# A four-layer convolution network on one core: first layer's window loads in four pieces, its outputs stored by group, its input loads in halves, the last layer's weight tables made later

## The reference, cut to what matters

```python
def _conv_reflect(x, w, bias, dil, pad):
    xp = jnp.pad(x, ((0, 0), (0, 0), (pad, pad), (pad, pad)), mode='reflect')
    out = jax.lax.conv_general_dilated(xp, w, window_strides=(1, 1), padding='VALID', rhs_dilation=(dil, dil), ...)
    return out + bias[None, :, None, None]

def _denoise_block(x, w1, b1, w2, b2, w3, b3, a, b, c):
    trip = _triplets(x)            # channels t-1, t, t+1
    ...
    o = a * _conv_reflect(xf, w1, b1, 1, 2) + b * _conv_reflect(xf, w2, b2, 2, 4) + c * _conv_reflect(xf, w3, b3, 4, 8)
    return jnp.tanh(o).reshape(B, T, H, W)
y = _denoise_block(x, blk1_...)
z = _denoise_block(y, blk2_...)
```

## Time and profile before

| | us |
|---|---|
| median of 3 runs | 5447.36 |
| fastest, slowest | 5419.58, 5452.12 |
| the profiled execution | 5428.8 |
| its span from the first to the last instruction | 5426.9 |
| TensorE busy in it | 5009.2 (92%) |
| VectorE busy | 3375.0 (62%) |
| ScalarE busy | 2396.5 (44%) |
| GpSimd busy | 1336.2 (25%) |

### The profile page before, as it was taken

How to read it: one execution, slowest core, us unless ns; L and a number is a source line. 1 busy time by engine, 2 the same in 40 slices (tenths; PEclk the granted TensorE clock), 3 DMA queues, 4 the chain that set the end, 5 groups by cost and what they waited for, 6 DMA issues and landing times. The chain is left out here.

```text
span 5426.9 us, 176472 instructions
## 1 busy us (share of the span) xinstructions
PE 5009.2 (92%) x78653; PEld 2747.5 (51%) x78653; DVE 3375.0 (62%) x6195; ACT 2396.5 (44%) x2999; POOL 1336.2 (25%) x1245
## 2 busy tenths in 40 slices
PE   4999999999999999999999997999677799999998
PEld 2444444445454555555544543443555566666665
DVE  4555554555543544444444445888899788888888
ACT  1222222222221111111111116785899698988997
POOL 0022222222221100000000000000677355555556
PEclk9999999999999999999999998999999999999999
DMA  8888889988977667667667667999688466666664
GB/s 241 228 236 261 245 244 251 260 237 258 255 216 209 192 188 201 180 178 205 177 175 203 179 183 245 328 325 319 242 307 310 142 148 152 152 151 152 151 151 121
DMA packets 328769, 1166.61 MB, mean 215 GB/s; under 512 B 49641, under 2 KB 50280, under 8 KB 276202
## 3 DMA queue, kind: packets, MB, share of 16 engines
q1 hardware_dynamic: 325848, 1152.94, 74.1%
q10 hardware_dynamic: 2162, 2.39, 0.2%
HBM read 683.58 MB, written 453.51 MB: 210 GB/s over the span
## 5 line engine op out<-in xcount | busy, mean ns | idle before, releaser
L679 PE MATMUL c_p<-c_w,wc 128*32 128x512 f16 x55296 | 3043.8, 380 | 130.3 <-issue 116.2
L679 PEld LDWEIGHTS c_p<-c_w,wc 128*32 128x32 f16 x55296 | 1551.3, 97 | 1594.2 <-issue 199.3
L739 ACT ACTIVATE c_t<-c_p,cbias,cscale 128x512 f32<-128x512 f32 x512 | 397.9, 777 | 2625.2 <-PE c_p L679 2625.2
L601 DVE TENSOR_TENSOR a_x<-c_t,a_x 128x512 f32<-128x512 f32 x256 | 181.1, 707 | 877.1 <-ACT c_t L739 865.2
L1697 PE MATMUL f_P<-f_qh,f_wt 64*64 64x512 f16 x4608 | 545.7, 378 | 1.8 <-DVE f_t L1593 1.8
L1697 PE MATMUL f_P<-f_hl,f_wt 64*64 64x512 f16 x4608 | 545.3, 379 | 0.0
L591 DVE TENSOR_SCALAR c_y<-c_t 128x512 f16<-128x512 f32 x256 | 116.7, 456 | 682.1 <-ACT c_t L739 681.9
L1858 POOL TENSOR_TENSOR f_y<-f_y,f_x 128x512 f32<-128x512 f32 x256 | 330.7, 1292 | 448.9 <-DVE f_hl L1572 442.8
L1593 DVE SCALAR_TENSOR_TENSOR f_t<-f_P,f_kk,f_ci 128x256 f32<-128x256 f32 x1024 | 423.4, 475 | 12.6 <-PE f_P L1697 7.3
L1457 POOL TENSOR_TENSOR e_hl<-e_g,e_hl 128x2048 f16<-128x2048 f32 x63 | 257.2, 4083 | 607.5 <-ACT e_hl L1407 607.5
L1658 PE MATMUL f_qp<-f_hil,f_gT 128*128 128x260 f16 (+1 forms) x3120 | 390.9, 275 | 4.0 <-DVE f_qh L1577 4.0
(11 more groups left out here) (263 smaller groups left out, 5981.7 us busy)
## 6 DMA issues: line engine op xcount, KB each, us to landing
c_w<-ys SPq DMA_DIRECT2D x144, 1056.0 KB, 11.9
c_w<-xs SPq DMA_DIRECT2D x140, 1056.0 KB, 12.2
d_x<-x SPq DMA_DIRECT2D x128, 1024.0 KB, 7.8
x<-d_x SPq DMA_DIRECT2D x128, 1024.0 KB, 5.1
ys<-c_y SPq DMA_DIRECT2D x576, 132.0 KB, 9.8
xs<-a_hl SPq DMA_DIRECT2D x70, 1056.0 KB, 9.7
a_x<-in_x SPq DMA_DIRECT2D x256, 256.0 KB, 10.1
a_x<-in_x SPq DMA_DIRECT2D x128, 512.0 KB, 4.6
```

What stands on the lines that cost most here:

```text
L679: t = p.matmul(pg[32 * j:32 * j + 32, :], wu[:, blk, wl, var, di, :], buf[:, bk, xl * PW + PAD + dx:xl * PW + PAD + dx + NW], start=(di == ...
L739: s.activation(tt_[n % 3][:, :], pp[:, n % 4, :], ACT.Tanh, bias=cbias[:, blk:blk + 1], scale=cscale[:, blk:blk + 1]).then_inc(c_act, 1)
```

## The change

Five edits, all in `layer0`:

1. `load(u, g)` loads a quarter of the window (four bands, 264 KB per DMA) and may start when TensorE is done with group g of unit u - 2. SP asks for it in group g of its iteration; in even units of block 1 all four are asked for at g = 3. TensorE still waits for all four at group 0.
2. `store_y(u, g)` stores group g of a unit as soon as its edges are mirrored: all four strips in one DMA per channel and place. The number of DMAs (eight or twelve per unit) and their size (132 KB) stay. GpSimd mirrors each group by itself.
3. `store_x1(u, g)` stores block 2's output by group, two DMAs of 128 KB instead of four of 256 KB per unit and 1 MB: eight per unit.
4. `load_x` is split into two halves of four DMAs, in the even and the odd unit of a pair.
5. `table_of(u)` = u - 60: the tables are made in units 60 to 123, and each is stored in the next unit.

```diff
-            return u - 8 if 0 <= u - 8 < 64 else None
+            return u - 60 if 0 <= u - 60 < 64 else None
...
-                    if u < NU:
-                        hv = yt[u % 2][:, :, :, :].rearrange("p r l w -> p (r l) w")
-                        q.wait_ge(c_lo, 4 * u + 4)
+                        if u < NU:
+                            hv = yt[u % 2][:, g]
+                            q.wait_ge(c_lo, 4 * u + g + 1)
...
-                def load(u):
+                def load(u, g):
                     if u >= 2:
-                        e.wait_ge(c_pe, 4 * (u - 1))
+                        e.wait_ge(c_pe, 4 * (u - 2) + g + 1)
...
-                            e.dma_start(win[half][gp % 2 + 2 * h8:128:4].rearrange("p k w -> p (k w)"),
-                                        dram(src, pair(b, gp, 0, 16 * half) + h8 * (8 * VP - RW), [[CP, 16], [RW, 2], [1, 16 * RW]])).then_inc(c_ld[half], 16)
+                            e.dma_start(win[half][gp % 2 + 2 * h8:128:4, 4 * g:4 * g + 4].rearrange("p k w -> p (k w)"),
+                                        dram(src, pair(b, gp, 0, 16 * half + 4 * g) + h8 * (8 * VP - RW),
+                                             [[CP, 16], [RW, 2], [1, 4 * RW]])).then_inc(c_ld[half] if u else c_l0[g // 2], 16)
...
-                def store_y(u):
-                    e.wait_ge(c_pad, 2 * (u + 1))
-                    for j in (0, 2, 1, 3):
-                        y = yt[u % 2][32 * j:32 * j + 32].rearrange("p r l w -> p r (l w)")
-                        for m, gp, slot in [(0, p, 1), (1, p + 1, 0)] + [(1, 0, 0)] * (p == 0) + [(0, 8, 1)] * (p == 7):
-                            e.dma_start(dram(ys, pair(b, gp, slot, 16 * half + j), [[VP, 16], [4 * RW, 4], [1, RW]]), y[m::2]).then_inc(c_yd[u % 2], 16)
+                def store_y(u, g):
+                    e.wait_ge(c_pad, 8 * u + 2 * g + 2)
+                    y = yt[u % 2][:, g].rearrange("p l w -> p (l w)")
+                    for m, gp, slot in [(0, p, 1), (1, p + 1, 0)] + [(1, 0, 0)] * (p == 0) + [(0, 8, 1)] * (p == 7):
+                        e.dma_start(dram(ys, pair(b, gp, slot, 16 * half) + g * 4 * RW, [[RW, 4], [VP, 16], [1, RW]]), y[m::2]).then_inc(c_yd[u % 2], 16)
...
+                def store_x1(u, g):
+                    for m in range(2):
+                        e.dma_start(dram(x1[b], (2 * p + m) * 4 * NW + (2 * half + g // 2) * NW + g % 2 * 64 * 4 * NC * NW,
+                                         [[4 * NC * NW, 64], [1, NW]]), xwin(u)[m::2, g]).then_inc(c_1d[u % 2], 16)
...
                 for u in range(2 * NU):
+                    late = u < NU and half == 0
                     for g in range(4):
                         i, s = stage_of(u, g)
                         if s == 3:
                             store_xs(i)
+                        if u + 2 < 2 * NU and not late:
+                            load(u + 2, g)
+                        if u + 2 < 2 * NU and late and g == 3:
+                            for gg in range(4):
+                                load(u + 2, gg)
+                        if blk:
+                            store_x1(u, g)
+                        else:
+                            store_y(u, g)
+                        if g == 0 and NU <= u + 1 < 2 * NU:
+                            load_res(u + 1)
+                        if g == 1 and u // 2 + 4 < NG:
+                            load_x(u // 2 + 4, (half,))
+                        if g == 2 and u and table_of(u - 1) is not None:
+                            store_table(table_of(u - 1))
```

More of the change, by code:

```diff
@@ L379, in n_win @@
         def n_win(u):
-            return 32 * sum(1 + (place(r)[2] == 0) for r in range(u % 2, u + 1, 2) if r)
+            return 128 * sum(1 + (place(r)[2] == 0) for r in range(u % 2, u + 1, 2) if r)
         def table_of(u):
-            return u - 8 if 0 <= u - 8 < 64 else None
+            return u - 60 if 0 <= u - 60 < 64 else None
         def xwin(u):
@@ L817, in load_x @@
                         e.wait_ge(a_lo, i - 1)
-                    for c, r in ((c, r) for c in range(2) for r in range(4)):
+                    for c, r in ((c, r) for c in channels for r in range(4)):
                         e.dma_start(xin[i % 2][:, c, NW * r:NW * r + NW],
@@ L832, in load @@
                     if u >= 2:
-                        e.wait_ge(c_pe, 4 * (u - 1))
-                    elif u == 1:
+                        e.wait_ge(c_pe, 4 * (u - 2) + g + 1)
+                    elif u == 1 and g == 0:
                         e.wait_ge(a_v, mark["wc"])
@@ L855, in load_res @@
                         e.wait_ge(c_mm, 8 * (r - 1))
-                        e.wait_ge(c_1d[u % 2], 64 * (r // 2))
+                        e.wait_ge(c_1d[u % 2], 128 * (r // 2))
                     else:
@@ L860, in load_res, with store_table @@
                         e.dma_start(xwin(u)[m::2], rows(x, u, m, NW, NH * NW)).then_inc(c_xd[u % 2], 16)
[L862 removed]
+                def store_y(u, g):
                     blk, b, p, half = place(u)
[L864 to L875 removed]
+                    e.wait_ge(c_pad, 8 * u + 2 * g + 2)
[3 more added lines that the diff above has]
+                def store_x1(u, g):
+                    e.wait_ge(c_lo, 4 * u + g + 1)
+                    blk, b, p, half = place(u)
+                    for m in range(2):
+                        e.dma_start(dram(x1[b], (2 * p + m) * 4 * NW + (2 * half + g // 2) * NW + g % 2 * 64 * 4 * NC * NW,
+                                         [[4 * NC * NW, 64], [1, NW]]), xwin(u)[m::2, g]).then_inc(c_1d[u % 2], 16)
+                def store_table(ht):
+                    e.wait_ge(w_t, 6 * (ht + 1))
+                    e.dma_start(K.wtab[ht], wt[ht % 2][:, :]).then_inc(w_td[ht % 2], 16)
                 load_x(0)
@@ L893, in _ @@
                 store_xs(1)
-                load(0)
-                load(1)
+                for u in range(2):
+                    for g in range(4):
+                        load(u, g)
                 load_x(3)
@@ L901, in _ @@
                     blk, b, p, half = place(u)
-                    nxt = (u + 1) // 2 + 2
+                    late = u < NU and half == 0
                     for g in range(4):
@@ L906, in _ @@
                             store_xs(i)
-                    if NU <= u + 1 < 2 * NU:
-                        load_res(u + 1)
-                    if u + 2 < 2 * NU:
-                        load(u + 2)
-                    if blk:
-                        store_x1(u)
-                    else:
-                        store_y(u)
-                    if table_of(u) is not None:
-                        ht = table_of(u)
-                        e.wait_ge(w_t, 6 * (ht + 1))
-                        e.dma_start(K.wtab[ht], wt[ht % 2][:, :]).then_inc(w_td[ht % 2], 16)
-                    if half == 0 and nxt + 2 < NG:
-                        load_x(nxt + 2)
+                        if u + 2 < 2 * NU and not late:
[13 more added lines that the diff above has]
+                            store_table(table_of(u - 1))
                 for q in range(2):
-                    e.wait_ge(c_1d[q], 64 * (NU // 2))
+                    e.wait_ge(c_1d[q], 128 * (NU // 2))
                     e.wait_ge(w_td[q], 16 * 32)
```

16 lines of the change are left out of this document (3 added, 13 removed).

## The result

| | before | after |
|---|---|---|
| median of 4 runs, us | 5437.55 | 5385.02 |
| lowest, highest | 5419.58, 5452.12 | 5374.08, 5391.84 |
| span of the profiled execution | 5426.9 | 5383.9 |
| block 1 (first activation of unit 0 to last of unit 63) | 1635.6 | 1659.3 |
| block 2 (to the last of unit 127) | 1569.2 | 1503.7 |

The ratio after to before is 0.990 (0.9879 to 0.992): 1.0% faster. 5507 us was forecast, 1.1% slower; the measured time lies in the range of 5380 to 5690 us, but the kernel got faster, not slower.

The account below looks back on a forecast made before the run. TensorE bounds both blocks before; after, four DMA engines were to bound block 1 at 1740 us. 5426.9 + 104 (block 1) - 45 (block 2) = 5486 us profiled, scaled to a 5507 us median; range 5380 to 5690 us.

Parts of the forecast that it names:

- What bounds the kernel: Both blocks: TensorE is the bound; undisturbed, block 1 could take 1562 us and block 2 1493 us.
- instruction fetches, delayed by long packets: Both blocks lose 74 and 76 us to fetch waits; window pieces were to win 45 us in block 2.
- Four of sixteen engines for the y stores: Block 1: slowest DRAM dimension 4 puts all y stores on the same four engines, 19.5 MB each.
- Their rates: Block 1, per engine: y stores 22.6 GB/s; other traffic 13.9 to 17.9 contended, perhaps 23.25 when the four lag.
- the two ends: Block 1, load of each of the four engines: 1910 us at contended rates, 1654 us at lone rates.
- The low end: Block 1: 863 us for y stores plus 791 us for the rest at 23.25 GB/s, 1654 us.
- TensorE stays the bound: Rival, chance 0.17: four engines need under some 1560 us, at 24.5 GB/s or more; faster, 5337 us.
- the contended rates: Block 1: rates measured with all sixteen engines in one kind of transfer; they give 1910 us on the four.
- The uneven load: Block 1, p = 0 and p = 7: extra stores and loads make two pairs need about 1.3 times their matmuls.
- Input halves, x1 by group, pads by group: Three edits predicted to bring nothing; a smaller x1 store landing last gives some 1 to 2 us, within rounding.
- Tables later: Tables leave block 1 but for its last four units; 448 KB per unit in block 2 costs nothing beyond the 45.
- The other twelve: Block 1: the twelve engines without four-wide y stores were said to need 1264 us.

Follow-up runs that it names:

- the version with wide stores: Changed kernel with y stores of a whole unit, sixteen wide, at group 3 as before: 5280.57 us, ratio 0.9702 to the kernel before.
- the pieces alone: Kernel before with each 1056 KB window DMA issued as four of 264 KB, same place and waits: 5290.14 us, ratio 0.9718.

## Why the prediction was right or wrong

- **What bounds the kernel: right.** 1562 and 1493 us were named for the undisturbed blocks, and the version with wide stores took 1562.1 and 1493.3.
- **The lost time is instruction fetches, delayed by long packets: right, and set too low.** -45 us were taken for block 2, -65.5 came, and -76 are there when no four-wide y store is in the way. The change's own block 2 keeps one wait of 6.9 us, in unit 65, where the last y stores of block 1 stand in front of a window; with the lower clock behind it this costs 10 us. In block 1 I let the fetch waits hide under a DMA bound that was not there; the pieces alone took 68 us off block 1.
- **Four of sixteen engines for the y stores: right.** 0.26 at four wide, 0.13 at two wide. It costs 255 us in the kernel before, and 74 in the changed one, 97 with the storing by group.
- **Their rates: wrong, and here the sign was lost.** The step is "these are the two ends. Both are above 1562 us, so TensorE can no longer be the bound of the whole block". The low end took 22.6 GB/s for the y stores and 23.25 for the rest. Alone at work, the four ran at 97 / 4 = 24.2 GB/s with y stores and at 105 / 4 = 26.2 with window packets among them. The window packets say the same: one of 8448 B lasts 324 ns there, 26.1 GB/s, where it lasted 491 ns in the median with sixteen engines at work. With the two rates an estimate of the load is 19.5/24.2 + 18.4/26.2 = 806 + 702 = 1508 us, under 1562; for the xs stores and the input no lone rate was read, and 26.2 stands in for them. By the y packets' own 91 ns for 2112 B (23.2 GB/s) the sum would be 840 + 702 = 1542 us, still under; the larger part of the error is then the 23.25 GB/s for the other traffic. TensorE stays the bound, as in the rival called "TensorE stays the bound", for whose turning point I had worked out 24.5 GB/s and which I gave 0.17. The trace of before had no lone rate of these kinds in my rows; the nearest, a store of eight engines ending the program, showed 23, and I made a floor of this one point. Then I went up a third of the way towards the contended rates (+86 us on top of 1654). These rates do not belong to engines that lag behind: 1659.3 us were measured where 1740 were forecast. That this lies within 5 us of the low end of 1654 is luck: the low end was a load of the four engines over the whole block, and the block's length is TensorE's 49.0 us a pair, with stalls in a few places.
- **The uneven load: right.** 1.3 times the matmuls' time for the two pairs at a change of image, hence about 30 us each. Measured: 26.8 us in units 16 to 19, 24.2 and 25.2 at the other two. Unit by unit against the version with wide stores, these are 76 of the 97 us between 1659 and 1562; the unit behind each cluster adds 8, the first three units of the block 10. I named it as what speaks against going lower, and did not work out that it alone would give 1562 + 3 x 30 = 1652 us.
- **Input halves, x1 by group, pads by group: nothing, not tried alone.** After's block 2 and that of the pieces alone differ by the 10 us in unit 65, so x1 by group costs nothing that shows.
- **Tables later: right in their kind, wrong beside the four engines.** I took their bytes out of the four engines' load. As the four were not the bound for most of the block by my later reading, I then expected 5 to 30 us from putting them back; it was 88. With their 1.6 MB the sum at lone rates is 1508 + 1.6/26.2 = 1569 us, above 1562: by this estimate they carry the kernel over the turning point, between the clusters too.
- **A slip in the sum.** "The other twelve need 1264 us" counts y stores for them, though all y stores were put on the four: 546 + 266 + 235 = 1047 us. Nothing in the forecast hangs on it.

Sum: +24 instead of +104 and -65 instead of -45. The signs of both terms were right; the first was over four times too large.

## What to carry to other kernels

Look at the slowest dimension of both sides of every DMA before merging transfers: with 4 there, three quarters of the DMA engines stand idle, and the share of a stretch tells it (0.26 here where such stores are alone). When an engine issues instructions without pause and waits now and then for nothing that the profile shows, shorten the packets of the large transfers; here this one edit was worth 2.8%. Those waits ended just behind a packet of the instruction queue. A bound from engines that work alone must be summed with rates of engines that work alone; if there is none in the trace, let the two ends lie on both sides of the turning point.

## What the hardware showed that I had not expected

- The gain of short packets is complete: from 94 us of fetch waits in 2600 us with 33.8-KB packets to 21 with 16.9-KB and none with 8.4-KB packets, at the same number of bytes.
- Few engines are quicker each. The same window packets that give 17.4 GB/s per engine with sixteen at work run beside y stores at 26 GB/s per engine with four at work. The small packets of the y stores gain far less: 91 ns for 2112 B in the median, both with sixteen engines at work (660 to 662 us in before) and with four (494 to 496 us in after). What holds the sixteen back was not tried.
- Two wide, the cost was linear to 0.5%: 2309 us for a sum of 2320.
